# Attention of a graph network on one core: weighted sums in four banks, row weights copied to SBUF, carries in the scores bank, scores and chunk steps spaced two rounds apart

## Chip, cores and metric

The kernel runs on one core of one Trainium2 chip. The metric is device time in microseconds (us), lower is better; a kernel's time is the median of its runs.

## What is computed

Two graph networks run one after the other on 3125 nodes and 100000 edges, sorted by their target node. The first has two message layers. The second has three attention layers (GATv2, four heads of 32 channels), and the change lies there. Cut to what matters:

```python
gl = (x @ Wl + bl).reshape(n, HEADS, CH)
gr = (x @ Wr + br).reshape(n, HEADS, CH)
xj = gl[src]
e = jax.nn.leaky_relu(xj + gr[dst] + edge_e, negative_slope=0.2)
alpha = jnp.einsum('ehc,hc->eh', e, att_w)
m = jax.ops.segment_max(alpha, dst, num_segments=n)
alpha = jnp.exp(alpha - m[dst])
denom = jax.ops.segment_sum(alpha, dst, num_segments=n)
out = jax.ops.segment_sum(xj * (alpha / (denom[dst] + 1e-16))[..., None], dst, num_segments=n)
```

A batch norm over nodes and a leaky rectifier follow each layer.

## The kernel before

The edges are cut into 812 tiles of 128, each of which belongs to one block of 112 target nodes. Four tiles are a quad, so a layer has 203 quads (`NQ`). Two tiles are a pair. Up to eight quads are a chunk: `ENDS` has their ends, 27 chunks a layer. The softmax runs as an online one over chunks: maxima are found inside a chunk with scans, carried on from the chunk before, and the sums that were already added are rescaled when the maximum rises.

Every engine's program is written out by hand as a loop over rounds `j`, one quad a round, and waits on semaphores alone; nothing reorders it. `STEPS[c]` has the rounds of chunk c's steps 0 to 4 (scans, carries, args on DVE; an exponential on ACT; the transposed weights on PE), `PXR[i]` the round in which quad i is weighted. What a round j holds:

- POOL (L581) gathers the rows of a tile's source nodes from DRAM, one indirect DMA a tile. It may be up to eight quads ahead of PE (a wait on `s_e`).
- SP loads, every second round, the one-hot and edge columns of eight tiles (`ste_d`, L804, 512 KB), the one-hot rows of an earlier pair of quads (`nbb_d`, L767, 224 KB) and, once a chunk, its masks (L788, L789). It is held back by `s_e` too.
- PE, in this order: the chunk steps (L1393 and L1394, L1399 and L1400, L1408 to L1411); `scat` of the quad that was weighted two rounds ago, two pairs (L1360, into `PS[6]` and `PS[7]`); `pair` (a transpose L1372 and a multiplication L1374 a tile, into `PS[0]` or `PS[1]`); `scores` of the quad before (L1385, into `PS[2]` or `PS[3]` by the chunk's parity). Each fp32 multiplication is two instructions.
- ACT: the expanders of quad j+2 (L1036), the one-hot rows of the weighted quad (L1042), the scaled copy LE of quad j (L1047), which waits for `pair(j)` and for the scores of quad j-2, and the chunk's exponentials (L1052).
- DVE: an addition (L1959), the weight step of a quad (`weight`, L2028: the gathered rows times the weights, 528 elements a partition), a second addition, the chunk step that is due, the leaked step (L2036, which waits for LE), and the third and fourth addition. An addition adds a tile's sums from PSUM to its node block in SBUF; the four of a round belong to the quad that PE summed in that round.

So `scat` of pair v waits for the additions of pair v-2, whose bank it overwrites:

```python
w.wait_ge(s_acc2, pair_at(l, v_ - 2) if v_ >= 2 else 0)
for t in (2 * v_, 2 * v_ + 1):
    x = e.matmul(PS[6 + v_ % 2][0:B, (t % 2) * 132:(t % 2 + 1) * 132], SQ4[:, i % 4, t % 4, :],
```

and `pair(j)` waits for the leaked step of quad j-2. The carries' small products stand in `PS[5]`, the transposed weights of a chunk in `PS[4]`, which the weight step reads from there. DVE also reads the block numbers of 16 tiles into registers once every four rounds (L509). Layer 2 has 19 further DVE steps (`prepared`, from L2040 on), one every sixth round.

## Time and profile before

| | us |
|---|---|
| median of 3 runs | 8436.67 |
| lowest and highest run | 8432.65, 8437.69 |
| profiled execution: span | 8424.8 |
| DVE busy | 3907.3 (46%) |
| ACT busy | 3352.0 (40%) |
| POOL busy | 4643.3 (55%) |
| PE busy, by modelled ends | 5601.5 (66%) |

The span goes from the first to the last instruction; of the profiled execution no other time is given, and the median lies 11.9 us above it. Times in the rows are counted from the span's start. The three attention layers' rounds lie at 4330 to 5650, 5688 to 7019 and 7057 to 8390 us. PE is the matmul, PEld the weight load, PEclk the granted clock of TensorE as a share of 2.4 GHz (0.5 is 1.2 GHz), mean over the stretch. In a row of the timeline "x4" are four instructions merged, and the brackets give the idle time before them and what ended it; "remote" means that no instruction ended shortly before the semaphore rose. Ends of matmuls are modelled.

### The profile page before, as it was taken

The numbers are of one execution on the slowest core, as the hardware profiler recorded it, in microseconds if no ns is written. First come the engines' busy times: TensorE is split into PE (matmuls) and PEld (weight loads), VectorE is DVE, ScalarE is ACT, GpSimd is POOL, SyncE is SP. The second block draws the span as 40 slices with busy tenths as digits, with TensorE's granted clock in tenths as the row PEclk, the third lists the DMA queues.
The fourth block names the chain that finished last, engine by engine and source line by source line (L and its number), as shares of the span: only waits on it lengthen the run. The fifth ranks groups of instructions, "written<-read, shape, count | busy, mean of one in ns | idle before, by whom it ended". The sixth has DMA issues, their size and how long they took to land.

```text
span 8424.8 us, 124432 instructions
## 1 busy us (share of the span) xinstructions
PE 5601.5 (66%) x35700; PEld 4989.9 (59%) x35700; DVE 3907.3 (46%) x13770; ACT 3352.0 (40%) x12652; POOL 4643.3 (55%) x4868
## 2 busy tenths in 40 slices
PE   7445445577777767777747777775766765777666
PEld 5333333566666666666646666665666665666666
DVE  4221221466666566665644444452444443444445
ACT  2222222366666556666623333332333332333332
POOL 2555554366666356666536666626666653666652
PEclk9999999899999888888978888877888886888887
DMA  2000001344344234444323333323333332333332
GB/s 56 22 25 23 24 22 21 95 105 103 103 105 103 78 102 121 119 118 119 101 54 111 109 107 108 108 78 94 107 103 108 107 107 66 111 104 108 107 106 64
DMA packets 489686, 743.92 MB, mean 88 GB/s; under 512 B 219285, under 2 KB 351865, under 8 KB 487973
## 3 DMA queue, kind: packets, MB, share of 16 engines
q1 hardware_dynamic: 307764, 423.98, 16.2%
q0 software_dynamic: 180928, 305.59, 15.1%
q10 hardware_dynamic: 320, 6.40, 0.3%
q8 instruction: 296, 4.85, 0.2%
q14 instruction: 378, 3.10, 0.1%
HBM read 636.97 MB, written 97.83 MB: 87 GB/s over the span
## 4 chain that ended last, share of the span: by engine, by line
PE 19%; issue 14%; another core or an unknown queue 12%; DVE 11%; ACT 4%; DVEq 3%; ACTq 0%; POOL 0%; DMA 0%
PE PS L1360 5%; DVE AR L1959 5%; PE PS L1374 4%; PE PS L1250 2%; PE PS L1372 2%; PE PS L1274 2%; PE PS L1271 1%; DVEq L509 1%; ACT AR L1047 1%; DVE AR L1879 1%; PE PS L1385 1%; DVEq L1959 1%; ACT AR L1036 1%; DVE AR L1793 1%
## 5 line engine op out<-in xcount | busy, mean ns | idle before, releaser
L581 POOL DMA_INDIRECT AR<-gtab_d,AR x2436 | 2309.8, 948 | 1554.0 <-issue 604.9
L573 POOL DMA_INDIRECT AR<-ptab_d,AR x1624 | 1548.1, 953 | 1030.0 <-issue 395.2
L1047 ACT ACTIVATE AR<-PS,AR 128x512 f32<-128x512 f32 x609 | 418.4, 687 | 2551.1 <-remote 1319.7
L1360 PE MATMUL PS<-AR 128*112 128x132 f32 x4872 | 943.5, 335 | 651.1 <-DVE AR L1959 636.9
L1360 PEld LDWEIGHTS PS<-AR 128*112 128x112 f32 x4872 | 742.1, 212 | 798.2 <-DVE AR L1959 485.7
L1959 DVE TENSOR_TENSOR AR<-AR,PS 112x132 f32 x2436 | 695.9, 286 | 1011.8 <-issue 401.4
L555 POOL DMA_INDIRECT rec_d<-AR x782 | 760.0, 972 | 661.6 <-DVE AR L1555 437.8
L1374 PE MATMUL PS<-AR 128*128 128x128 f32 x4872 | 1058.1, 319 | 20.0 <-issue 19.5
L2036 DVE SCALAR_TENSOR_TENSOR AR<-PS,AR 128x512 f32<-128x512 f32 x609 | 455.7, 748 | 1201.5 <-issue 702.3
L1374 PEld LDWEIGHTS PS<-AR 128*128 128x128 f32 x4872 | 924.9, 236 | 23.2 <-issue 22.9
L1250 PE MATMUL PS<-AR 128*112 128x161 f32 x3248 | 672.5, 335 | 356.9 <-DVE AR L1879 216.6
L1385 PE MATMUL PS<-AR 128*128 128x128 f32 x4872 | 740.4, 298 | 152.3 <-DVE AR L2036 87.0
L950 ACT ACTIVATE AR<-PS 128x160 f32<-128x160 f32 x1624 | 493.6, 304 | 795.1 <-remote 334.2
L1271 PE MATMUL PS<-AR 112*128 x3248 | 789.7, 327 | 25.8 <-issue 25.4
L1879 DVE TENSOR_TENSOR AR<-AR,PS 112x161 f32 x1624 | 520.2, 320 | 618.0 <-issue 264.6
L1372 PE MATMUL PS<-ident,AR 128*128 128x128 f32 x2436 | 778.9, 320 | 40.6 <-DMA AR<-gtab_d,AR 20.8
L1274 PE MATMUL PS<-AR,ident 128*128 128x160 f32 x3248 | 777.9, 323 | 2.4 <-issue 2.4
L1385 PEld LDWEIGHTS PS<-AR 128*128 128x128 f32 x4872 | 683.1, 215 | 152.4 <-DVE AR L2036 93.4
L1250 PEld LDWEIGHTS PS<-AR 128*112 128x112 f32 x3248 | 526.6, 199 | 409.3 <-issue 390.9
L1103 PE MATMUL PS<-AR 128*56 128x168 bf16 (+3 forms) x1369 | 379.6, 432 | 461.3 <-DVE AR L1569 319.1
L1271 PEld LDWEIGHTS PS<-AR 112*128 112x128 f32 x3248 | 598.0, 212 | 43.0 <-issue 42.7
L1274 PEld LDWEIGHTS PS<-AR,ident 128*128 128x128 f32 x3248 | 595.1, 211 | 2.0 <-issue 1.9
(344 smaller groups left out, 8790.5 us busy)
## 6 DMA issues: line engine op xcount, KB each, us to landing
AR<-ste_d SPq DMA_DIRECT2D x404, 512.0 KB
AR<-nbb_d SPq DMA_DIRECT2D x303, 224.0 KB
ste_d<-AR SPq DMA_DIRECT2D x101, 512.0 KB
AR<-gtab_d,AR POOLq DMA_INDIRECT x2436
AR<-ptab_d,AR POOLq DMA_INDIRECT x1624
nbb_d<-AR SPq DMA_DIRECT2D x101, 224.0 KB
AR<-key_d SPq DMA_DIRECT2D x94, 224.0 KB
AR<-rec_d SPq DMA_DIRECT2D x812, 8.0 KB
```

The source lines that it names most:

```text
L555: e.indirect_dma_start(out=rec_d[:, :], out_offset=bass.IndirectOffsetOnAxis(ap=rowi[:, n:n + 1], axis=0), in_=REC[:, c * RW:(c + 1) * RW] ...
L573: e.indirect_dma_start(out=XJ1[:, t % 32, :], out_offset=None, in_=tabs_d[0][:, :], in_offset=off).then_inc(done_, 16)
L581: e.indirect_dma_start(out=xj2(t)[:, t % 4, :], out_offset=None, in_=tabs_d[1][:, :], in_offset=off).then_inc(done_, 16)
L1250: x = e.matmul(PS[4 + v_ % 2][0:B, (t % 2) * 161:(t % 2 + 1) * 161], SW[:, (t // 4) % 4, t % 4, :], VB[:, v_ % 6, t % 2, :], start=True, s ...
L1271: e.matmul(o, STE[0:B, ste_slot(l, t), (t % 8) * 128:(t % 8 + 1) * 128], TABQ[0:B, bass.ds(block_of(cp, "tensor", t), 1), :], start=True, ...
L1274: x = e.matmul(o, ident[:, :], XJ1[:, t % 32, :], start=False, stop=True, skip_group_check=True)
L1360: x = e.matmul(PS[6 + v_ % 2][0:B, (t % 2) * 132:(t % 2 + 1) * 132], SQ4[:, i % 4, t % 4, :], PX[:, i % 5, t % 4, :, :].rearrange("p c h - ...
L1372: e.transpose(o, xj2(t)[:, t % 4, 0:128], ident[:, :])
L1374: x = e.matmul(o, expander(t), STE[:, ste_slot(l + 2, t), (t % 8) * 128:(t % 8 + 1) * 128], start=False, stop=True, skip_group_check=True)
L1385: x = e.matmul(PS[2 + c % 2][:, 0:128], ATW[:, 31 - t:159 - t], LE[:, i % 2, kk * 128:(kk + 1) * 128], start=(t == 0), stop=(i == ENDS[c] ...
L1879: x = e.tensor_tensor(o, o, PS[4 + v_ % 2][0:B, (t % 2) * 161:(t % 2 + 1) * 161].unsqueeze(1), ALU.add)
L1959: x = e.tensor_tensor(o, o, PS[6 + v_ % 2][0:B, (t % 2) * 132:(t % 2 + 1) * 132].rearrange("p (a c h) -> p a c h", a=1, h=4), ALU.add)
```

## The change

Line numbers of the changed kernel differ by a few from those above (L1385 becomes L1388, L1360 L1363, L1372 L1375, L1374 L1377, L1959 L1960, L2028 L2037, L2036 L2045).

- `scat` writes to `PS[4]` to `PS[7]` in turn, and waits for the additions of pair v-4.
- The carries' products and the transposed weights go to the columns behind and over the scores in the chunk's scores bank `PS[2 + c % 2]`.
- The first weight step of a chunk copies the transposed weights to `PTT` and the rescaling factors to `RT`, both in SBUF, and gives the bank back through a new semaphore `s_tc`. `scores` waits for that instead of for the args of chunk c-2. All weight steps read `PTT`, the rescaling reads `RT`.
- `scores(j - 2)` stands at the end of round j, where `scores(j - 1)` stood.
- The rounds of the chunk steps: 9, 10, 11, 11, 12 for chunk 0 become 9, 11, 13, 13, 15, and so on every eight rounds. Quads are weighted 15 rounds behind their tiles' round where it was 12, and two a round near the end of a layer, where DVE calls `weight` twice. There are 26 chunks, and 215 rounds where there were 217.
- SP loads `nbb_d` two steps of its loop later.

```diff
-    ends = list(range(8, 185, 8)) + [190, 195, 199, NQ]
+    ends = list(range(8, 193, 8)) + [198, NQ]
...
-        back = max(turn + 3, px[-1] + 1 if px else 0)
-        steps.append((turn, turn + 1, turn + 2, turn + 2, back))
-        px += [back + i for i in range(end - start)]
+        back = turn + 6
+        for i in range(start, end):
+            back = max(back, px[-1] + 1 if px and (px[-1] < NQ or px[-2:] == [px[-1]] * 2) else px[-1] if px else 0)
+            px.append(back)
+        steps.append((turn, turn + 2, turn + 4, turn + 4, px[start]))
...
-                for g8 in range(NG + 7):
+                for g8 in range(NG + 9):
...
-                    w.wait_ge(s_acc2, pair_at(l, v_ - 2) if v_ >= 2 else 0)
+                    w.wait_ge(s_acc2, pair_at(l, v_ - 4) if v_ >= 4 else 0)
                     for t in (2 * v_, 2 * v_ + 1):
-                        x = e.matmul(PS[6 + v_ % 2][0:B, (t % 2) * 132:(t % 2 + 1) * 132], SQ4[:, i % 4, t % 4, :],
+                        x = e.matmul(PS[4 + v_ % 4][0:B, (t % 2) * 132:(t % 2 + 1) * 132], SQ4[:, i % 4, t % 4, :],
...
-                        w.wait_ge(s_arg, chunk_at(l, c - 2))
+                        w.wait_ge(s_tc, chunk_at(l, c - 2))
...
                         w.wait_ge(s_pt, chunk_at(l, c))
-                        w.wait_ge(s_rs, chunk_at(l, c - 1))
-                        w.wait_ge(s_px, quad_at(l, chunk_start(c) - 1))
-                        e.transpose(PS[4][:, 0:128], PT, ident[:, :])
+                        e.transpose(PS[2 + c % 2][:, 0:128], PT, ident[:, :])
...
-                    if 1 <= j <= NQ:
-                        scores(j - 1)
+                    if 2 <= j <= NQ + 1:
+                        scores(j - 2)
...
-                    w.wait_ge(s_r, chunk_at(l, chunk_of(i)))
+                    c = chunk_of(i)
+                    t0 = 4 * (i - chunk_start(c))
+                    if t0 == 0:
+                        w.wait_ge(s_r, chunk_at(l, c))
+                        if c or l:
+                            w.wait_ge(s_px, quad_at(l, i - 1))
+                            w.wait_ge(s_rs, chunk_at(l, c - 1))
+                        v(e.tensor_copy(RT, PS[2 + c % 2][0:B, 128:132]))
+                        done(e.tensor_copy(PTT, PS[2 + c % 2][:, 0:128]), s_tc)
+                        w.wait_ge(s_tc, chunk_at(l, c))
...
-                        PS[4][:, 0:128].rearrange("p (h t) -> p t h", h=4)[:, t0:t0 + 4, :].unsqueeze(2).to_broadcast([128, 4, 33, 4]),
+                        PTT.rearrange("p (h t) -> p t h", h=4)[:, t0:t0 + 4, :].unsqueeze(2).to_broadcast([128, 4, 33, 4]),
...
                     add()
+                    if len(quads) > 1:
+                        weight(quads[1])
```

PE, layer 0, around the small products of a chunk's carries, with the banks' numbers. Before:

```order
L1374 MATMUL PS0<-AR 128x128
L1385 MATMUL PS2<-AR 128x128 x4
L1399 MATMUL PS5<-ones,AR 128x1
L1400 MATMUL PS5<-ones,AR 128x1
L1360 MATMUL PS6<-AR 112x132 x2
L1360 MATMUL PS7<-AR 112x132 x2
L1372 MATMUL PS1<-ident,AR 128x128
```

With the change:

```order
L1377 MATMUL PS0<-AR 128x128
L1388 MATMUL PS2<-AR 128x128 x4
L1402 MATMUL PS3<-ones,AR 128x1
L1403 MATMUL PS3<-ones,AR 128x1
L1363 MATMUL PS4<-AR 112x132 x2
L1363 MATMUL PS5<-AR 112x132 x2
L1375 MATMUL PS1<-ident,AR 128x128
```

The small products moved from `PS5` to the chunk's scores bank `PS3`, and the two pairs of weighted sums of a round from `PS6` and `PS7` to `PS4` and `PS5` (the next round takes `PS6` and `PS7`).

DVE, layer 0, around the first weight step of a chunk (528 elements); the additions have 132, and an ISA row sets an address for the next. Before:

```order
L1959 ISA
L1959 TENSOR_TENSOR AR<-AR,PS6 112x132
L2028 TENSOR_TENSOR AR<-AR,PS4 128x528
L1959 ISA
L1959 TENSOR_TENSOR AR<-AR,PS6 112x132
L2036 SCALAR_TENSOR_TENSOR AR<-PS0,AR 128x512
```

With the change:

```order
L1960 ISA
L1960 TENSOR_TENSOR AR<-AR,PS4 112x132
L2032 COPY AR<-PS2 112x4
L2033 COPY AR<-PS2 128x128
L2037 TENSOR_TENSOR AR<-AR 128x528
L1960 ISA
L1960 TENSOR_TENSOR AR<-AR,PS4 112x132
L2045 SCALAR_TENSOR_TENSOR AR<-PS1,AR 128x512
```

Two copies from the scores bank stand ahead of the multiplication, and its second input is no longer in PSUM.

## Rows read from the trace of the kernel before

**Rows 1.** Timeline, layer 0: start us, us, engine, line and operation, tiles, count, idle before.
```profile
4999.56 0.64 PE L1374 MATMUL PS<-AR 128*128 128x128 f32 x2
...
4999.99 1.86 PE L1385 MATMUL PS<-AR 128*128 128x128 f32 x8
...
5000.36 0.69 ACT L1047 ACTIVATE AR<-PS,AR 128x512 f32<-128x512 f32 x1 [3.30 <-issue]
...
5001.08 0.75 DVE L2036 SCALAR_TENSOR_TENSOR AR<-PS,AR 128x512 f32<-128x512 f32 x1 [2.52 <-ACT AR L1047]
...
5002.18 0.29 DVE L1959 TENSOR_TENSOR AR<-AR,PS 112x132 f32 x1 [0.15 <-issue]
...
5002.53 0.70 PE L1360 MATMUL PS<-AR 128*112 128x132 f32 x4 [0.23 <-DVE AR L1959]
...
5004.18 0.39 PE L1374 MATMUL PS<-AR 128*128 128x128 f32 x2
...
5004.40 1.06 PE L1385 MATMUL PS<-AR 128*128 128x128 f32 x8
5006.95 0.29 DVE L1959 TENSOR_TENSOR AR<-AR,PS 112x132 f32 x1 [4.48 <-remote]
5007.04 0.69 ACT L1047 ACTIVATE AR<-PS,AR 128x512 f32<-128x512 f32 x1 [4.74 <-remote]
...
5009.59 0.29 DVE L1959 TENSOR_TENSOR AR<-AR,PS 112x132 f32 x1 [0.22 <-DVE AR L1959]
```

**Rows 2.** Waits of all engines: who for whom, us in total, times, longest us.
```profile
ACT AR L1047 <- remote: 1319.7, 279, 38.4
...
PE PS L1360 <- DVE AR L1959: 636.9, 384, 5.0
```

**Rows 3.** Waits of PE, the chunk steps.
```profile
PE PS L1408 <- ACT AR L1052: 129.7, 59, 5.4
...
PE PS L1393 <- DVE AR L1973: 102.4, 26, 4.6
```

**Rows 4.** Windows: us; busy of PE, PEld, DVE, ACT, POOL; PEclk, DMA share, GB/s.
```profile
4487.10:5600.10 1113.00, 813.99 (x5406) 755.41 (x5405) 512.12 (x1519) 364.57 (x1130) 664.99 (x702) 0.85 0.37 106
5600.10:5650.20 50.10, 35.37 (x160) 29.87 (x158) 30.15 (x100) 9.34 (x19) 0.00 (x0) 0.60 0.23 68
5847.80:6969.40 1121.60, 795.05 (x5405) 734.36 (x5404) 510.21 (x1518) 364.68 (x1130) 663.03 (x700) 0.86 0.37 105
7213.40:8338.00 1124.60, 793.06 (x5406) 730.41 (x5405) 522.80 (x1538) 365.03 (x1130) 667.23 (x702) 0.87 0.37 105
```

**Rows 5.** Windows with L1372 alone: us; busy and count of PE, PEld.
```profile
4487.10:5600.10 1113.00, 232.37 (x728) 124.75 (x729) 0.85 0.37 106
```

**Rows 6.** Timeline of POOL, start of layer 1.
```profile
5706.30 0.95 POOL L581 DMA_INDIRECT AR<-gtab_d,AR  x1 [0.30 <-issue]
...
5732.56 0.95 POOL L581 DMA_INDIRECT AR<-gtab_d,AR  x1 [0.30 <-issue]
```

**Rows 7.** Timeline, layer 2, around a DVE step with both inputs in SBUF.
```profile
7483.23 0.95 POOL L581 DMA_INDIRECT AR<-gtab_d,AR  x1 [0.30 <-issue]
...
7483.77 1.08 DVE L2048 TENSOR_TENSOR AR<-AR 112x896 f32<-112x896 f32 x1
...
7484.48 1.20 POOL L581 DMA_INDIRECT AR<-gtab_d,AR  x1 [0.30 <-issue]
```

**Rows 8.** Timeline of DVE, the carries and args of one chunk.
```profile
5019.70 0.27 DVE L1983 COPY AR<-PS 1x128 f32<-1x128 f32 x1
...
5022.01 0.15 DVE L2004 TENSOR_TENSOR AR<-AR 1x4 f32<-1x4 f32 x1
...
5025.56 0.15 DVE L2011 COPY AR<-PS 128x2 f32<-128x2 f32 x1
...
5026.92 0.29 DVE L2020 TENSOR_TENSOR AR<-PS,AR 128x128 f32<-128x128 f32 x1
```

**Rows 9.** Chain of waits, 5016 to 5019 us: start us, us, what.
```profile
5017.42 1.10 DVEq L509
```

More of the change, by code:

```diff
@@ L222, in gnn_program @@
         NW, FD, FR = carve(4, 1), carve(4, 1), carve(4, 1)
+        PTT, RT = carve(128), carve(4, B)
         assert cur[0] <= AREA - 4 * T - TK - NB, cur[0]
@@ L380, in gnn_program @@
             sem(n) for n in ("s_ex", "s_s0", "s_v", "s_car", "s_c", "s_arg", "s_pt", "s_f", "s_r"))
-        s_px, s_oh2, s_scat2, s_acc2, s_rs = (sem(n) for n in ("s_px", "s_oh2", "s_scat2", "s_acc2", "s_rs"))
+        s_px, s_oh2, s_scat2, s_acc2, s_rs, s_tc = (sem(n) for n in ("s_px", "s_oh2", "s_scat2", "s_acc2", "s_rs", "s_tc"))
         s_cnt, s_lk, s_k4, s_kx, s_mk = (sem(n) for n in ("s_cnt", "s_lk", "s_k4", "s_kx", "s_mk"))
@@ L758, in sync_program @@
                             load_masks(e, w, l, c)
-                    o8 = g8 - 7
+                    o8 = g8 - 9
                     if o8 >= 0:
@@ L1392, in tensor_program @@
                         w.wait_ge(s_s0, chunk_at(l, c))
-                        e.matmul(PS[5][0:1, 128:256], SS[:, 0:1], ident[:, :], start=True, stop=True, skip_group_check=True)
-                        done(e.matmul(PS[5][0:1, 256:384], SS[:, 127:128], ident[:, :], start=True, stop=True, skip_group_check=True), s_v)
+                        e.matmul(PS[2 + c % 2][0:1, 128:256], SS[:, 0:1], ident[:, :], start=True, stop=True, skip_group_check=True)
+                        done(e.matmul(PS[2 + c % 2][0:1, 256:384], SS[:, 127:128], ident[:, :], start=True, stop=True, skip_group_check=True), s_v)
                     c = step_of(j, 2)
@@ L1398, in tensor_program @@
                         w.wait_ge(s_car, chunk_at(l, c))
-                        e.matmul(PS[5][:, 384:385], GL_, ones[0:1, 0:1], start=True, stop=True, skip_group_check=True)
-                        done(e.matmul(PS[5][:, 385:386], GE_, ones[0:1, 0:1], start=True, stop=True, skip_group_check=True), s_c)
+                        e.matmul(PS[2 + c % 2][:, 384:385], GL_, ones[0:1, 0:1], start=True, stop=True, skip_group_check=True)
+                        done(e.matmul(PS[2 + c % 2][:, 385:386], GE_, ones[0:1, 0:1], start=True, stop=True, skip_group_check=True), s_c)
                     c = step_of(j, 4)
@@ L1405, in tensor_program @@
                         w.wait_ge(s_pt, chunk_at(l, c))
-                        w.wait_ge(s_rs, chunk_at(l, c - 1))
-                        w.wait_ge(s_px, quad_at(l, chunk_start(c) - 1))
-                        e.transpose(PS[4][:, 0:128], PT, ident[:, :])
+                        e.transpose(PS[2 + c % 2][:, 0:128], PT, ident[:, :])
                         w.wait_ge(s_f, chunk_at(l, c))
-                        e.matmul(PS[4][0:B, 128:132], MR[:, mask_slot(l, c), 512:624], FR, start=True, stop=False, skip_group_check=True)
-                        done(e.matmul(PS[4][0:B, 128:132], MR[:, mask_slot(l, c), 624:736], ones[0:1, 0:4],
+                        e.matmul(PS[2 + c % 2][0:B, 128:132], MR[:, mask_slot(l, c), 512:624], FR, start=True, stop=False, skip_group_check=True)
+                        done(e.matmul(PS[2 + c % 2][0:B, 128:132], MR[:, mask_slot(l, c), 624:736], ones[0:1, 0:4],
                                       start=False, stop=True, skip_group_check=True), s_r)
@@ L1978, in carries @@
                     g4, e4 = GL_.rearrange("p (h t) -> p h t", h=4), GE_.rearrange("p (h t) -> p h t", h=4)
-                    v0, v1 = PS[5][0:1, 128:256], PS[5][0:1, 256:384]
+                    v0, v1 = PS[2 + c % 2][0:1, 128:256], PS[2 + c % 2][0:1, 256:384]
                     w.wait_ge(s_v, chunk_at(l, c))
@@ L1983, in carries @@
                     v(e.tensor_copy(vr[:, :, 1:33], v1.rearrange("p (h t) -> p h t", h=4)))
-                    ends_ = v(e.tensor_tensor(BE_, PS[5][0:1, 129:257], r[:, 256:384], ALU.add))
+                    ends_ = v(e.tensor_tensor(BE_, PS[2 + c % 2][0:1, 129:257], r[:, 256:384], ALU.add))
                     add()
@@ L2010, in args @@
                     w.wait_ge(s_v, chunk_at(l, c))
-                    columns = v(e.tensor_copy(CC, PS[5][:, 384:386]))
+                    columns = v(e.tensor_copy(CC, PS[2 + c % 2][:, 384:386]))
                     add()
```

7 lines of the change are left out of this document (3 added, 4 removed).

## The prediction

> **What bounds the kernel now.** I read the waits first, then the timeline of a few rounds, then windows over whole layers. The waits [rows 2] name the place: TensorE (PE) stood idle for 636.9 us, in 384 waits, before the weighted sums L1360, until VectorE (DVE) had done an addition L1959. The biggest entry of all is ACT's: 279 of its 609 LE steps (L1047) waited 1319.7 us for something "remote".
>
> The timeline [rows 1] shows both inside one loop. The pair's last multiplications L1374 start at 5004.18 and end at 5004.57; the LE step starts at 5007.04, so PE's completion reached ACT 2.5 us late, and DVE's addition at 5006.95 had waited as long. This is what "remote" stands for. One round earlier the same step was prompt: L1374 ended at 5000.20, LE started at 5000.36. From there LE to the leaked step L2036 takes 0.72 us, from that to the end of the fourth addition 1.39 (5001.08 to 5002.47), and at once, at 5002.53, PE starts the second pair of sums. PE cannot run ahead: with two banks the second pair of sums of a round needs the additions behind the previous round's leaked step. So one round closes a loop: sums, pairs, LE, leaked, additions, sums.
>
> The pace: a window with L1372 alone [rows 5] holds 728 of them, four a round, so 182 rounds; the three middles of the layers [rows 4] take 1113.0 + 1121.6 + 1124.6 = 3359.2 us for 546 rounds, **6.15 us a round**. In them no engine is full: POOL 665 of 1113, DVE 512, PE 814 by modelled ends. The floor under it: when nothing holds POOL, gathers start 26.26 us apart over 21 gathers [rows 6], 1.25 each, **5.0 us a round** of four.
>
> **The change, part by part.**
>
> *Four banks.* Sums of pair v wait for the additions of v-4, so both pairs of a round need only additions of two rounds before. The 636.9 us [rows 2] lose their cause; what is late next is this loop over two rounds, at full clock: second sums, pairs and scores on PE 2.93 us (5002.53 to 5005.46 [rows 1]); lateness of the completion, 279 of 609 times some 2.5 and otherwise 0.16, mean 1.23; LE to leaked 0.72; leaked to the fourth addition's end 1.39. Together 6.3 us for two rounds. No instruction is added or removed here.
>
> *Scores two rounds behind.* Same instructions, later. PE no longer waits at its round's end for the leaked step of the round before. But LE(j) may overwrite its buffer only after scores(j-2), and these now stand behind pair(j): every LE starts at the scores' end, 0.9 us behind the pair's end (5005.46 against 5004.57), and at half clock 1.65 (5001.85 against 5000.20). I have put the scores inside the 2.93, so this new wait is paid. Behind LE on ACT are the next expanders, wanted by PE only three rounds later: hidden.
>
> *Chunk steps two rounds apart, carries in the scores bank.* PE waited at L1408 129.7 us and at L1393 102.4 [rows 3], because ACT and DVE had one round for a step. Now they have two; I take these waits as gone. The scores bank is given back at the first weight step of the chunk, round 8c+15, and wanted by the scores of chunk c+2 in round 8c+18: three rounds of cover, 15 us. If the cover were gone, PE would wait once a chunk for DVE. On DVE the steps stay, before the leaked step: carries 5019.70 to 5022.16, args 5025.56 to 5027.21 [rows 8], 2.46 + 1.65, the scans taken like the args, 5.8 a chunk. Twice a chunk the block numbers are loaded to registers, 1.10 each [rows 9].
>
> *Row weights copied to SBUF.* Two DVE copies a chunk and one own wait. The copy at 5019.70 took 0.27 [rows 8]; two of them and a gap make 0.2 to 0.8, I take 0.5, hidden in DVE's slack: 78 chunks, 39 us of work that counts only if DVE becomes the bound. The multiplication itself keeps its 528 elements; its second input now comes from SBUF. A row for that form is the added step L2048: 896 elements with both inputs in SBUF took 1.08 us, and the gather that POOL started inside it took 1.20 us against 0.95 [rows 7]. So each of the 609 multiplications may cost POOL between nothing and 0.25 us; with POOL short of being the bound it costs nothing, and I take nothing. The Trainium skill, page "SBUF — State Buffer", section "Who interferes with whom", has a rule that speaks against the change here: a DVE instruction with two SBUF inputs contends with a GpSimd instruction that reads SBUF. By that rule the fastest outcome would be 7968 us instead of 7832 (both worked out below), and the forecast stays, since its pace lies above both. By that rule, the trace agrees in the one place shown.
>
> *Weighted sums three rounds later, two a round at the end.* After the last tile round 15 quads remain where 12 did. Before, this tail took 50.1 us (from 5600.1 to 5650.2 [rows 4]). DVE needs 2.64 us a quad when it never waits (5006.95 to 5009.59 [rows 1]), so 3 x 2.64 x 3 layers = +24 us; bounds 0 (the doubled rounds hide each other's waits) and 24. On SP the nbb load comes two pairs of rounds later and a mask load one; they are issued behind the same loads of ste_d, at least three rounds before use: hidden. One chunk fewer a layer (27 to 26) saves about 6 us of DVE work each, hidden as well, taken as 0.
>
> **The sum.** At full clock: the two-round loop 6.3, the chunk's work on DVE (5.8 + 0.5 + 2.2) / 8 x 2 = 2.1, together 8.4, or 4.2 a round: below POOL's 5.0, so POOL sets the pace. At half clock PE's own work decides: 28 instructions a round at 0.213 us (two from 4999.56 to 4999.99 [rows 1]) are 5.96, with ten small ones a chunk 6.2. The granted clock is 0.85 to 0.87 [rows 4], so some 30% of the time is at 1.2 GHz and the rest at 2.4. With that share kept: 0.7 x 5.0 + 0.3 x 6.2 = 5.36, taken as **5.4 us a round**. Saved: 546 x (6.15 - 5.4) = 411 us. I leave the first 20 rounds of each layer as they are, and add 24 for the tail. The profiled span 8424.8 becomes 8038; the median of the runs lies 11.9 above the span, so **8050 us**.
>
> **The rivals.**
>
> 1. *POOL's pace throughout.* The eight quads that POOL is ahead even out the half-clock rounds: 5.0 a round, 8437 - 629 + 24 = 7832 us. For it: 702 gathers at 1.25 are 878 of the 1113 us, so POOL lacks little, and PE would be busy without long gaps, which may hold 2.4 GHz. Against: completions 2.5 us late stay. 0.19.
> 2. *POOL's pace, lengthened by the multiplications from SBUF.* Each of the 609 holds one gather for up to 0.25 us: 5.25 a round, 7968 us. For it: the 1.20 us gather. Against: a gather is held only if it starts while the multiplication runs. The page named above has this rule. 0.10.
> 3. *The late completions take the place of the bank wait.* They hold ACT, DVE and POOL at once; if DVE cannot catch up in between (it has 2.64 + 1.1 of work a round, more in chunk steps), the pace ends near 5.8: 8437 - 192 + 24 = 8268 us. 0.17.
> 4. *Nothing moves.* The LE step behind the scores gives back what the banks free: 6.15 a round, 8437 to 8460 us. 0.05.
> 5. *Slower: PE at half clock.* In the middles PE works in bursts and is granted 0.85 to 0.87; in the tail, where its work is thin, 0.60 [rows 4]. If PE's work, spread evenly, is granted 1.2 GHz all along, PE is the bound in its own order, at 6.24 a round with nothing lost between: +48 + 24, 8509 us. It decides once more than 90% of the time is at 1.2 GHz, a PEclk under 0.55 in the middles. Against: such a PE has no gaps, and behind gapless work the level went from half to full between 5001.85 and 5002.53 [rows 1]. 0.09.
>
> **How the numbers follow.** Forecast 0.40 (5.2 to 5.6 a round, 7940 to 8160), rivals 0.19, 0.10, 0.17, 0.05, 0.09. A measurement of this kernel tells some 0.2% (17 us) from no change. Faster by more: 0.40 + 0.19 + 0.10 + 0.17 = 0.86. Rival 4 mostly stands within: same 0.04, slower 0.10. The range leaves out rivals 4 and 5 and a little at each end: its low end is rival 1 with the first rounds quickened too (36 rounds x 1.15 = 41 less), 7790; its high end a pace of 5.85, 8300.
>
> **What the profile after would show.** Right: the wait of L1360 for L1959 below 150 us, the chunk steps' waits on PE below 60; "remote" before the LE step still there; 728 transposes in about 980 us; gathers 1.25 apart in full-clock stretches; PEclk not under 0.85. Rival 1 shows as gathers 1.25 apart through the middles, rival 2 as gathers of 1.2 us beside the multiplications, rival 3 as DVE and ACT idle together for "remote" while PE waits for the additions again, rival 5 as PEclk near 0.5. The forecast is wrong in its main step if PE still waits for DVE's additions for more than 400 us.

## The result, and the profile after

The changed kernel took **8347.51 us** (median of 4 runs, 8335.14 to 8353.35) against 8437.18 of the kernel before on the same chip (4 runs, 8432.65 to 8448.02): ratio **0.9886, 95% interval 0.9874 to 0.9898**. That is 1.1% faster. The forecast was 8050 us, and its range ended at 8300.

Lines have moved by the edit: the sums L1360 are L1363 now, the transposes L1372 are L1375, the pair's multiplications L1374 are L1377, the scores L1385 are L1388, the additions L1959 are L1960, the weight step L2028 is L2037, the leaked step L2036 is L2045, LE L1047 is L1050, the gathers L581 are L584.

The costliest groups on the page of the changed kernel, its first line with them:

```profile
span 8333.0 us, 124313 instructions
...
L584 POOL DMA_INDIRECT AR<-gtab_d,AR x2436 | 2583.5, 1061 | 1193.9 <-issue 673.3
...
L1050 ACT ACTIVATE AR<-PS,AR 128x512 f32<-128x512 f32 x609 | 417.9, 686 | 2337.3 <-remote 1777.0
...
L2037 DVE TENSOR_TENSOR AR<-AR 128x528 f32<-128x528 f32 x609 | 654.8, 1076 | 2.9
```

Its waits of PE (us, times, longest), which answer to [rows 2, 3]:

```profile
PE PS L1363 <- issue: 298.0, 366, 2.5
...
PE PS L1363 <- DVE AR L1960: 68.4, 91, 2.1
...
PE PS L1409 <- ACT AR L1055: 20.3, 17, 2.8
...
PE PS L1396 <- DVE AR L1974: 2.8, 4, 1.3
```

Windows over the same stretches as [rows 4] (first transposes of quads 20 to 202 of each layer, and one tail); the columns are those of [rows 4]:

```profile
4479.60:5567.30 1087.70, 833.76 (x5398) 750.54 (x5396) 581.40 (x1551) 366.38 (x1136) 766.14 (x707) 0.81 0.39 109
5567.30:5628.30 61.00, 40.43 (x196) 35.10 (x194) 45.29 (x132) 11.34 (x24) 0.00 (x0) 0.65 0.22 63
5817.80:6902.00 1084.20, 843.91 (x5398) 757.64 (x5397) 580.85 (x1551) 366.17 (x1136) 757.34 (x706) 0.82 0.39 110
7150.70:8235.40 1084.70, 827.49 (x5398) 746.84 (x5397) 589.78 (x1564) 365.50 (x1136) 753.89 (x705) 0.82 0.38 110
```

What these show. The waits for the additions fell from 636.9 us to 68.4, and PE's wait for ACT's exponential from 129.7 to 20.3, as meant. But the middles went only from 3359.2 to 3256.6 us, 5.96 us a round for 6.15. Three things grew that no instruction count explains. Two are durations: the weight step's multiplication, from 697 ns (the group of L2028 on the page of the kernel before) to **1076 ns** at the same 528 elements, and the gathers, from 948 to **1061 ns** on average.

The third is idle time of PE for which the profile shows no releaser ("issue"). PE's waits from 4450 to 5600 us, in layer 0, before the change and after it:

```profile
PE PS L1360 <- DVE AR L1959: 201.6, 113, 4.0
PE PS L1408 <- ACT AR L1052: 31.7, 16, 2.6
PE PS L1399 <- issue: 26.7, 14, 2.1
```

```profile
PE PS L1363 <- issue: 101.7, 121, 2.5
PE PS L1377 <- issue: 48.3, 88, 1.7
PE PS L1375 <- issue: 32.1, 46, 2.6
PE PS L1388 <- issue: 22.8, 44, 1.1
PE PS L1363 <- DVE AR L1960: 17.6, 21, 2.1
```

Summed over the three middles, PE's idle time put down to VectorE or ScalarE fell from 847 us to 57, and the idle time without a releaser rose from 103 to **680**. Some of those 680 us are still waits for other engines, since only 818 of the additions' 1218 semaphore updates are in this trace: 128 us end right behind an instruction of VectorE or ScalarE. But 385 us, in 588 gaps, stand ahead of instructions that wait for no semaphore at all; before the change that was 37 us in 50. PE stands still between its own instructions.

The time by stretch: middles -103, first twenty rounds of the three layers -21, tails, from the last such transpose to the last addition (49.7, 49.5, 50.1 before, 61.1, 58.8, 61.1 after) +32: together -92, and the spans differ by 91.8.

A timeline of the changed kernel shows a held gather and a late completion within four microseconds: a gather that starts inside a multiplication takes twice its time (5013.19), and LE starts 1.59 us behind the recorded end of the scores it waits for (5012.92 to 5014.51, "remote"):

```profile
5011.23 1.69 PE L1388 MATMUL PS<-AR 128*128 128x128 f32 x8
...
5011.95 0.94 POOL L584 DMA_INDIRECT AR<-gtab_d,AR  x1 [0.30 <-issue]
...
5013.16 1.08 DVE L2037 TENSOR_TENSOR AR<-AR 128x528 f32<-128x528 f32 x1
5013.19 1.88 POOL L584 DMA_INDIRECT AR<-gtab_d,AR  x1 [0.30 <-issue]
...
5014.51 0.69 ACT L1050 ACTIVATE AR<-PS,AR 128x512 f32<-128x512 f32 x1 [1.95 <-remote]
```

### The profile page after: what moved, and what is told of

It reads as the page before. It is cut to its first block, busy times and chain, and to the rows that moved or that the text cites. A ratio compares the mean times of both kernels' runs of the same rounds, so it can differ in the third digit from the quotient of the medians.

```text
span 8333.0 us, 124313 instructions
## 1 busy us (share of the span) xinstructions
PE 5688.3 (68%) x35659; PEld 5004.8 (60%) x35659; DVE 4136.5 (50%) x13855; ACT 3352.7 (40%) x12645; POOL 4908.0 (59%) x4868
## 4 chain that ended last, share of the span: by engine, by line
PE 30%; issue 13%; another core or an unknown queue 8%; DVE 7%; ACT 4%; DVEq 1%; ACTq 0%; DMA 0%; POOL 0%
PE PS L1363 7%; PE PS L1377 6%; PE PS L1388 6%; PE PS L1375 3%; PE PS L1253 2%; PE PS L1277 1%; PE PS L1274 1%; DVE AR L1880 1%; DVE AR L1960 1%; ACT AR L1039 1%; DVE AR L1794 1%; ACT AR L953 1%; DVE AR L1889 1%; ACT AR L1050 1%
## 5 line engine op out<-in xcount | busy, mean ns | idle before, releaser
L584 POOL DMA_INDIRECT AR<-gtab_d,AR x2436 | 2583.5, 1061 | 1193.9 <-issue 673.3
L1050 ACT ACTIVATE AR<-PS,AR 128x512 f32<-128x512 f32 x609 | 417.9, 686 | 2337.3 <-remote 1777.0
L1377 PE MATMUL PS<-AR 128*128 128x128 f32 x4872 | 1097.2, 320 | 152.7 <-issue 148.1
L1363 PE MATMUL PS<-AR 128*112 128x132 f32 x4872 | 898.1, 318 | 386.4 <-issue 298.0
L1377 PEld LDWEIGHTS PS<-AR 128*128 128x128 f32 x4872 | 923.4, 232 | 214.1 <-issue 212.4
L2045 DVE SCALAR_TENSOR_TENSOR AR<-PS,AR 128x512 f32<-128x512 f32 x609 | 455.0, 747 | 1159.9 <-ACT AR L1050 910.5
L1960 DVE TENSOR_TENSOR AR<-AR,PS 112x132 f32 x2436 | 692.2, 284 | 654.3 <-PE PS L1363 246.6
L1363 PEld LDWEIGHTS PS<-AR 128*112 128x112 f32 x4872 | 720.3, 203 | 483.6 <-issue 378.2
L1375 PE MATMUL PS<-ident,AR 128*128 128x128 f32 x2436 | 769.9, 316 | 252.9 <-issue 133.7
L1388 PE MATMUL PS<-AR 128*128 128x128 f32 x4872 | 819.5, 312 | 113.1 <-issue 109.2
L1388 PEld LDWEIGHTS PS<-AR 128*128 128x128 f32 x4872 | 741.9, 227 | 144.7 <-issue 141.5
L1253 PEld LDWEIGHTS PS<-AR 128*112 128x112 f32 x3248 | 520.6, 197 | 408.0 <-issue 388.7
L2037 DVE TENSOR_TENSOR AR<-AR 128x528 f32<-128x528 f32 x609 | 654.8, 1076 | 2.9
```

Of the source, the lines that this page charges most:

```text
L584: e.indirect_dma_start(out=xj2(t)[:, t % 4, :], out_offset=None, in_=tabs_d[1][:, :], in_offset=off).then_inc(done_, 16)
L1253: x = e.matmul(PS[4 + v_ % 2][0:B, (t % 2) * 161:(t % 2 + 1) * 161], SW[:, (t // 4) % 4, t % 4, :], VB[:, v_ % 6, t % 2, :], start=True, s ...
L1363: x = e.matmul(PS[4 + v_ % 4][0:B, (t % 2) * 132:(t % 2 + 1) * 132], SQ4[:, i % 4, t % 4, :], PX[:, i % 5, t % 4, :, :].rearrange("p c h - ...
L1375: e.transpose(o, xj2(t)[:, t % 4, 0:128], ident[:, :])
L1377: x = e.matmul(o, expander(t), STE[:, ste_slot(l + 2, t), (t % 8) * 128:(t % 8 + 1) * 128], start=False, stop=True, skip_group_check=True)
L1388: x = e.matmul(PS[2 + c % 2][:, 0:128], ATW[:, 31 - t:159 - t], LE[:, i % 2, kk * 128:(kk + 1) * 128], start=(t == 0), stop=(i == ENDS[c] ...
```

## The experiments

Theories: (1) PE itself is the bound, 28 instructions at 0.213 us being just 5.96; (2) the longer multiplications and gathers eat the gain; (3) PE's completions come late by a fixed delay a round; (4) the LE step's new wait for the scores eats it. Variants have letters: 1b says that the gathers set the pace where PE completes promptly, 1c that PE with its halts is the bound where it does not. The runs fell on several chips, and that turned out to matter more than any edit: on one the kernel before took 8367 us, on four others 6731 to 6735, a fifth less, with the same instructions. I call them **slow chips** (the first one, 8437, and that one) and **quick chips**. Whether it is the chip or its condition at that hour is not shown: each of the two slow chips was met once. Ratios are always to the kernel before on the same chip.

**PE by itself, quick chip.**

> TensorE by itself: six sections of 20 groups of 28 fp32 instructions (A 128x128 weights and 128 columns, B transposes, C 112 rows and 132 columns, D 4 columns, E the mix of one round of the attention loop, F one weight tile for all), each group's end told by a semaphore to a one-column ScalarE activation, whose starts show when groups are really complete; the output is a copy of the input and nothing of the reference is computed. Theory 1 (TensorE sustains one fp32 instruction in about 0.213 us whatever granted clock the rows show, since 5.96 us a round in the changed kernel is 28 x 0.213): the groups of E complete 5.96 us apart, although rows of single matmuls may start 0.11 us apart. Theory 2 (the extra time of the vector multiplication and the gathers, 1076 against 697 ns and 1061 against 948 ns, sets the pace, and TensorE has room): groups of E complete about 28 x 0.11 to 28 x 0.13, 3.1 to 3.7 us apart, at a high granted clock.

The whole took 441.3 us. At a granted clock of 1.0 a group in the round's mix (E) ended every 3.13 us, 0.112 an instruction; the section with four moving columns was granted 0.5 and took 5.97 us a group, 0.213. So 0.213 is the price at 1.2 GHz and no hidden limit. Theory 1 in its first form does not hold on such a chip.

**Scores issued twice, and a third LE buffer, quick chip.**

```diff
-                        for kk in range(4):
+                        for kk in (0, 0, 1, 1, 2, 2, 3, 3):
```

> The changed kernel with every scores matmul issued twice (the scores come out doubled, so the output differs), 8 TensorE instructions more a round, 36 for 28. Theory 1 (TensorE is the bound at 0.213 us an instruction): 8 x 0.213 = 1.70 us more a round, x 609 rounds = about 1040 us, 9385 us in all (9250 to 9450). Theory 2 (GpSimd and the vector port set the pace, 5.44 us a round of gathers within 5.96): TensorE has room at 0.11 to 0.12 us an instruction, under 100 us more. Theory 3 (late completions: a fixed delay in each round): about 8 x 0.11 x 609 = 540 us more.

```diff
-        LE = carve(2 * 512).rearrange("p (g n) -> p g n", g=2)
+        LE = carve(3 * 512).rearrange("p (g n) -> p g n", g=3)
...
-                        if j >= 2:
-                            w.wait_ge(s_lin, quad_at(l, j - 2))
+                        if j >= 3:
+                            w.wait_ge(s_lin, quad_at(l, j - 3))
```

> The changed kernel with a third buffer for the activations LE, so that the activation of round j waits for the scores of round j-3 and no longer for those of j-2, which now stand behind the pair of round j. Theory 1 (TensorE bound): within 20 us of the changed kernel, 8330 to 8370. Theory 4 (this wait, 378 waits and 1777 us idle of ScalarE in the changed kernel, holds the loop): the start of the activation comes back from 5.4 us to about 1.7 us behind the pair's end and the pace falls towards 5.44 us a round, -250 to -320 us, about 8060 us.

Measured: 7050.3 and 7023.9 us, where the change itself takes 7028.8 (below). Eight more PE instructions a round cost 21 us in all, and LE starting at once behind the pair gains nothing. PE and the LE wait are not the bound there. The first number is what theory 2 asked (under 100 us more), and the gain that theory 4 asked of the second is absent.

**Three banks, weights read from PSUM.** PS[4] to PS[6] hold the sums, PS[7] the transposed weights, and the copy is gone:

```diff
-                    w.wait_ge(s_acc2, pair_at(l, v_ - 4) if v_ >= 4 else 0)
+                    w.wait_ge(s_acc2, pair_at(l, v_ - 3) if v_ >= 3 else 0)
...
-                        PTT.rearrange("p (h t) -> p t h", h=4)[:, t0:t0 + 4, :].unsqueeze(2).to_broadcast([128, 4, 33, 4]),
+                        PS[7][:, 0:128].rearrange("p (h t) -> p t h", h=4)[:, t0:t0 + 4, :].unsqueeze(2).to_broadcast([128, 4, 33, 4]),
```

> The changed kernel with three banks for the weighted sums and the transposed weights kept in the eighth bank of PSUM and read from there, no copy to SBUF. Theory 2 (two SBUF inputs of the vector multiplication against GpSimd): the multiplication falls from 1076 to about 700 ns and the gathers from 1061 to about 950 ns, and the time falls with the gathers by up to 4 x 0.11 x 609 = 270 us, to about 8080. Theory 1 (TensorE bound): the two durations fall in the same way, and the time stays within 30 us of the changed kernel, 8320 to 8380.

It ran four times, each on a quick chip (6745, 6746, 6736, 6741 us): ratios 1.0017, 1.0016, 1.0013 and 1.0016, the last 1.0006 to 1.0027. Both durations fell as expected, the multiplication to 696 ns and the gathers to 948. The theories differed in the time, and on a quick chip it fell by 284 us against the change's 7028.8 (below), near the 270 of theory 2.

**The change itself, on a quick chip**, was run late, on the same chip as the fourth of those:

> The changed kernel unaltered, which has so far run only where the kernel before takes 8437 or 8367 us (ratios 0.989 and 0.985). Where the kernel before takes 6733 us: gathers back to back, 0.951 us where no multiplication overlaps them and 1.33 where one does, 4 x (1.07 + 0.305) = 5.5 us a round, 7025 to 7060 us, ratio 1.045, its neighbours with one edit having taken 7024, 7040 and 7062. Where it takes 8367 or more: 0.985 to 0.989 again.

7028.84 us against 6731.02: **1.0447, 1.0425 to 1.0469. On this quick chip the change is 4.5% slower.** Windows over 182 rounds of layer 0, of the change and then of the three-bank kernel:

```profile
3518.10:4512.40 994.30, 762.58 (x5397) 697.97 (x5395) 579.15 (x1548) 367.58 (x1136) 773.36 (x726) 0.89 0.44 121
```

```profile
3517.20:4424.10 906.90, 717.30 (x5397) 657.50 (x5396) 502.15 (x1502) 367.12 (x1136) 685.92 (x725) 0.94 0.47 133
```

Gathers: 773.36 / 726 = 1.065 us, with 0.305 between them, (994.30 - 773.36) / 726; 4 x 1.37 = 5.48 a round, and the window has 5.46. Of the three-bank kernel: 0.946 + 0.305, 5.0, and 4.98. POOL is the bound from end to end in both. PE's waits for gathered rows say the same, first in the change on this quick chip, then in the change on the first, slow one:

```profile
PE PS L1375 <- DMA AR<-gtab_d,AR: 817.9, 700, 6.9
```

```profile
PE PS L1375 <- DMA AR<-gtab_d,AR: 26.2, 26, 6.7
```

On the slow chip the rows lie ready. From the end of a quad's last gather instruction to PE's first transpose of that quad it is 34 us on average and never under 19 in the middles (32 and 12 on the second slow chip), where it is 0.0 us on average on the quick one. POOL is 6.5 quads ahead of PE there and 1.1 here, and in the slow middle of layer 0 it is POOL that waits, 105 us, for PE (L1377 or "remote"). So the gathers set the pace on quick chips, and on slow chips they do not.

The timeline on the quick chip shows the price again, and LE prompt behind the scores' end, 4002.54:

```profile
4000.44 1.07 DVE L2037 TENSOR_TENSOR AR<-AR 128x528 f32<-128x528 f32 x1
4000.71 1.63 POOL L584 DMA_INDIRECT AR<-gtab_d,AR  x1 [0.30 <-issue]
...
4001.48 1.06 PE L1388 MATMUL PS<-AR 128*128 128x128 f32 x8
...
4002.63 0.69 ACT L1050 ACTIVATE AR<-PS,AR 128x512 f32<-128x512 f32 x1 [3.41 <-PE PS L1388]
```

Over the whole trace, the 790 gathers that overlap a multiplication take 1.286 us and the other 1646 take 0.951.

**The copy alone, slow chip (8367 us).**

```diff
+                        v(e.tensor_copy(RT, PS[4][0:B, 128:132]))
+                        done(e.tensor_copy(PTT, PS[4][:, 0:128]), s_tc)
...
-                        PS[4][:, 0:128].rearrange("p (h t) -> p t h", h=4)[:, t0:t0 + 4, :].unsqueeze(2).to_broadcast([128, 4, 33, 4]),
+                        PTT.rearrange("p (h t) -> p t h", h=4)[:, t0:t0 + 4, :].unsqueeze(2).to_broadcast([128, 4, 33, 4]),
```

> The kernel before with one part of the change alone: the transposed weights and the carry's factor are copied from their PSUM bank to SBUF, and the vector multiplications read them there; two banks for the sums, and all steps as before. Theory 2 (two SBUF inputs of the multiplication hold up GpSimd's gathers): the multiplication takes 1076 us for 697 ns, the gathers 1.06 to 1.07 for 0.95 us. Where gathers stand back to back that is 4 x 0.12 x 609 = 290 us more, +4.3%, 7025 us; where the kernel before takes 8437 us, its slack of 0.29 us behind each gather takes it up, and the time moves by less than 100 us. Without that contention: no difference on either.

(The first "us" behind 1076 stands for ns.) Multiplication 1077 ns, gathers 1054 on average; time 8393.59 us, ratio 1.0025 (1.0006 to 1.0043). So the copy alone brings both prices; in a kernel whose gathers have slack they cost 26 us (5 to 36).

**The change and the kernel before again, and PE alone, on that slow chip.**

> The changed kernel unaltered. The last four runs shared a chip on which the kernel before took 6733 us, not 8437, and TensorE by itself completed 28 instructions in 3.13 us. Theory 1b (two limits: where TensorE completes promptly, the gathers set the pace in every case, and the change makes each gather 0.12 us longer, 4 x (1.07 + 0.305) = 5.5 us a round against 4 x (0.948 + 0.305) = 5.0): on such a chip the changed kernel takes about 7030 us, 4.4% over the kernel before. Where the kernel before takes 8437 us again, the ratio of the first comparison, 0.989, comes again. Theory 3 (the time of the change is the same on both chips): 0.989 on either.

> The kernel before, unaltered, for its profile beside the others of this call. Theory 1b: on a chip with 6733 us its gathers stand back to back, 0.95 us and 0.305 us apart, 5.0 us a round, and the two-round loop through the sums of TensorE and the additions of VectorE, 6.3 us a round on the first chip, does not hold it; where it takes 8437 us, the profile is that of before, 6.15 us a round.

> TensorE by itself once more, the same six sections (nothing of the reference is computed). On a chip where the kernel before takes 6733 us: 3.13 us for 28 instructions at full clock, 5.97 at half, as before. On a chip where it takes 8437 us, theory 1 (TensorE by itself sustains less there, whatever clock the rows show): 5.9 us or so at a granted clock near 1; theory 5 (TensorE alone is as quick there, and something beside it, DMA or the other engines, delays its completions): 3.13 us again.

8252.84 us, ratio 0.9851 (0.9832 to 0.9871): the first result came again, a little larger. The kernel before shows the trace of [rows 1 to 4] again, 6.14 us a round. PE alone took 441.5 us, with the same 3.13 and 5.97 us a group: by itself PE is as quick on a slow chip. Inside the kernels it is not. In a window of 900 us from 4500 on, the share of PE's recorded semaphore updates that come over 0.5 us behind the last recorded end of an instruction that makes them is 45% in the kernel before and 59% in the change on this chip (41% and 68% on the first one), and none in the change on a quick chip. The median late one is 1.8 to 3.1 us behind. In the first 200 us of the program a fifth of the updates are late already, long before the attention layers. The idle time of PE without a releaser is there again too, 714 us in the change's middles for 48 in those of the kernel before.

**PE beside the other engines.**

> TensorE with the instruction mix of one round (28 fp32 instructions a group, 40 groups a section; nothing of the reference is computed), eight sections: alone; beside VectorE multiplications; beside ScalarE activations; beside GpSimd gathers; beside SyncE's 512 KB loads; beside all four; with a wait for its own semaphore after each group, alone; and so beside all four. On a chip where the kernel before takes 8350 to 8440 us, TensorE's semaphores come up to 13 us late in half to three quarters of the updates. Theory 5a (the halts come with the power or traffic of the other engines): no halts alone, halts of 2 to 7 us in one or more of the sections beside others, which names the engine. Theory 5b (the halts come where TensorE stops and starts): they show in the two sections with waits and in no other. Theory 5c (neither): 3.13 us a group in all. On a chip where the kernel before takes 6733 us: 3.13 us a group in all sections without the wait.

> TensorE with the instruction mix of one round, eight sections of 40 groups: alone; beside VectorE; beside ScalarE; beside GpSimd's gathers; beside SyncE's loads; beside all four; waiting for its own semaphore after each group, alone; and so beside all four (nothing of the reference is computed). On the chip where the kernel before takes 6734 us it took 1039 us in all with no late semaphore. On a chip where the kernel before takes 8350 to 8440 us: theory 5a (the halts come with the power or traffic of other engines): halts of 2 to 7 us in one or more of the sections beside others and none alone, 1100 to 1500 us in all. Theory 5b: only in the two sections with waits. Theory 5c (neither, something that these sections do not have): 1039 us again.

Both runs fell on quick chips: 1038.8 and 1040.1 us, 3.13 us a group in all sections without the wait and 3.44 in the two with it. What brings the halts on slow chips was not reached by them and stays open. One row answers another question: its multiplications have two contiguous SBUF operands of the size of L2037, and gathers beside them,

```profile
L89 POOL DMA_INDIRECT G<-in_x,idx x270 | 254.9, 944 | 754.3 <-PE PS L48 382.9 <-ACT A L116 290.0 <-issue 81.4
L103 DVE TENSOR_TENSOR V<-VI 128x528 f32<-128x528 f32 x330 | 205.8, 704 | 762.0 <-PE PS L48 762.0
```

take 704 and 944 ns, also where both run. Two SBUF operands alone are not what costs 1076.

**The copy laid out the other way, quick chip.** The same copy, with the four heads of a tile side by side:

```diff
-                        done(e.tensor_copy(PTT, PS[2 + c % 2][:, 0:128]), s_tc)
+                        done(e.tensor_copy(PTT.rearrange("p (t h) -> p t h", h=4), PS[2 + c % 2][:, 0:128].rearrange("p (h t) -> p t h", h=4)), s_tc)
...
-                        PTT.rearrange("p (h t) -> p t h", h=4)[:, t0:t0 + 4, :].unsqueeze(2).to_broadcast([128, 4, 33, 4]),
+                        PTT.rearrange("p (t h) -> p t h", h=4)[:, t0:t0 + 4, :].unsqueeze(2).to_broadcast([128, 4, 33, 4]),
```

> The changed kernel with the copy to SBUF laid out by tile and head instead of by head and tile (the copy itself reads PSUM with the stride), so that the multiplication reads four neighbouring elements at a time instead of elements 128 bytes apart; nothing else is altered. In the runs so far a multiplication of two contiguous SBUF operands of the same 128x528 size took 701 to 707 ns beside gathers of 944 ns, while the change's own takes 1080 ns and the gathers that overlap it 1332 ns (951 where they don't), so theory 2c (the stride of the SBUF operand, not its being in SBUF, costs the 380 ns and holds up GpSimd) expects 700 ns and gathers of 0.95 us: where the kernel before takes 6733 us, 6735 to 6760 instead of about 7030; where it takes 8367, 7950 to 8050 if the gathers hold the changed kernel there, 8200 to 8250 if TensorE with its halts does. Theory 2 (two SBUF inputs as such, or the broadcast): 1076 ns and 1.07 us stay, and the time stays at about 7030 or 8253.

6855.57 us, ratio 1.0186 (1.0165 to 1.0207), neither of the two values expected. Its groups:

```profile
L584 POOL DMA_INDIRECT AR<-gtab_d,AR x2436 | 2421.3, 994 | 864.2 <-issue 715.5
...
L2037 DVE TENSOR_TENSOR AR<-AR 128x528 f32<-128x528 f32 x609 | 426.3, 701 | 2.9
```

The multiplication is back at 701 ns, so its 370 to 380 ns were all stride; the gathers that overlap it still take 1.106 us for 0.949. So the change's price on a quick chip has two parts: of its +298 us the stride makes some 173 (7029 to 6856), and the gathers still held make most of the rest, which the contiguous multiplication did not show. Whether that comes from the broadcast operand or from something else that the kernel has and that small program lacks was not tested.

**Half the scores, and two banks, quick chip.**

> The changed kernel with two of the four scores matmuls of each round left out (the attention scores are wrong, 24 TensorE instructions a round for 28). Where the kernel before takes 6733 us and the gathers stand back to back: no change, 7030 us. Where it takes 8367: theory 1c (TensorE with its halts is the bound, 5.9 us for 28 instructions, halted a third of the time): 4 x 0.21 = 0.84 us a round less until the gathers' 5.53 bound it, so 5.55 us a round, -210 us, 8040 us. Theory 4 (the wait of the activation for the scores holds the loop): -4 x 0.11 x 609 = -270 us at most, through the same line. Theory 2 (gathers alone bound it): within 40 us of 8253.

Then two banks:

```diff
-                    w.wait_ge(s_acc2, pair_at(l, v_ - 4) if v_ >= 4 else 0)
+                    w.wait_ge(s_acc2, pair_at(l, v_ - 2) if v_ >= 2 else 0)
...
-                        x = e.matmul(PS[4 + v_ % 4][0:B, (t % 2) * 132:(t % 2 + 1) * 132], SQ4[:, i % 4, t % 4, :],
+                        x = e.matmul(PS[6 + v_ % 2][0:B, (t % 2) * 132:(t % 2 + 1) * 132], SQ4[:, i % 4, t % 4, :],
```

> The changed kernel with two banks for the sums again, the wait for the additions of the pair before the last back; the copy to SBUF, the later scores and the later chunk steps stay. Where the kernel before takes 8367 us: the step of the prediction (four banks take away 637 us of waits of TensorE, up to 0.9 us a round) says 8253 + 250 to 400; if TensorE's halts absorb the waits, as the changed kernel's gain of 1.5% suggests, +50 to +120 us, 8300 to 8370. Where it takes 6733: 7030, no change, since the gathers bound both.

7039.69 us (one run): PE's work is free there. Two banks took 7061.73, ratio 1.0488 (1.0471 to 1.0506). The wait for the additions is all there again,

```profile
PE PS L1363 <- DVE AR L1960: 636.7, 590, 2.8
```

and it costs 33 us against the 7028.84 of the change, measured on another chip. That the total is that of before the change [rows 2] is chance: it is 590 waits here and 384 there, on a slow chip. A wait of the engine that is not the bound has its full size in the list and next to no price.

**The banks alone.** The kernel before with a third bank for the sums and the edge rows and carries in the scores bank; nothing else:

```diff
-                    w.wait_ge(s_acc2, pair_at(l, v_ - 2) if v_ >= 2 else 0)
+                    w.wait_ge(s_acc2, pair_at(l, v_ - 3) if v_ >= 3 else 0)
...
-                        x = e.matmul(PS[6 + v_ % 2][0:B, (t % 2) * 132:(t % 2 + 1) * 132], SQ4[:, i % 4, t % 4, :],
+                        x = e.matmul(PS[(4, 6, 7)[v_ % 3]][0:B, (t % 2) * 132:(t % 2 + 1) * 132], SQ4[:, i % 4, t % 4, :],
```

> The kernel before with one part of the change alone, as far as it goes without the copy: a third bank for the sums (the wait of TensorE for the pair two earlier becomes one for the pair three earlier), got by moving the edge rows and carry columns into the bank of the scores; weights read from PSUM, scores one round behind and chunk steps one round apart as before. Where the kernel before takes 6733 us and the gathers stand back to back: no change, 6720 to 6750. Where it takes 8367 or 8437: if TensorE's waits for the additions are the limit there (theory of the prediction), the gathers' slack of 0.29 us each closes in large part, -150 to -350 us, 8020 to 8220 of 8367; if its halts are (theory 1c), the waits only change their name, 0 to -100 us.

A quick chip once more: 6728.1 us, ratio 0.9990 (0.9981 to 1.0000). The tail took 48.2 us in layer 0, against 56.1 in the three-bank kernel with the later chunk steps, so the later steps cost about 8 us a layer in the tail. The third and fourth runs of the three-bank kernel asked about slow chips,

> Three banks for the sums, transposed weights read from PSUM, no copy, the later scores and chunk steps of the change kept: the same kernel as twice before, 6745 us on a chip where the kernel before takes 6734 us. Where the kernel before takes 8367 us: theory 2b (the copy's longer gathers and multiplications are what holds the changed kernel at 5.93 us a round, 5.53 of it gathers): the gathers fall to 0.948 us and the pace towards 5.4 to 5.5, -250 to -300 us against the changed kernel's 8253, 7950 to 8000. Theory 1c (TensorE with its halts is the bound at 5.9): 8230 to 8290.

> Three banks, transposed weights read from PSUM, no copy, the later scores and chunk steps kept. Where the kernel before takes 6733 us: 6736 to 6746, as three times before. Where it takes 8367 or more: theory 2b (the copy's longer gathers hold the changed kernel at 5.93 us a round): 250 to 300 us under the changed kernel of the same call. Theory 1c (TensorE with its halts holds it): within 40 us of it.

and got a quick chip's 6735.94 and 6741.34 (the second run had asked the same, and got 6745.80). No kernel tried beats the kernel before on a quick chip by more than the measurement tells: those that read the weights from PSUM end at POOL's 5.0 us a round.

## Why the prediction was wrong

Point by point, by its own steps:

- *Four banks: the 636.9 us lose their cause.* The wait went, 68.4 left, under the 150 that it named. The time did not go with it.
- *Chunk steps' waits gone.* Right: 20.3 us for ACT and 2.8 for DVE remain of 129.7 and 102.4.
- *"4.2 a round: below POOL's 5.0, so POOL sets the pace"*, in the 70% of the time at full clock. **This is the step that failed.** On this chip POOL never set the pace: it stood 6.5 quads ahead of PE, and PE waited for gathered rows 26.2 us in the whole kernel. PE itself set it. In the three middles PE was busy 2505 us by modelled ends, idle 680 us with no releaser shown and idle 57 us for VectorE and ScalarE; that is 3242 of the 3256.6 us, or 4.6, 1.24 and 0.10 us a round. The sum had no term for the 1.24. It counted a late completion once in a loop of two rounds, at 1.23 us on average, and put PE's own standing still at nothing.
- *Where the 411 us went.* In the middles the profile shows 790 us less of PE waiting for other engines. 576 us came back as idle time without a releaser (up to 128 of them unrecorded waits, as said above), and 103 us as longer work of PE, whose granted clock fell from a range of 0.85 to 0.87 to one of 0.81 to 0.82. What is left over is about the 103 us that the middles gained. Either the wait for the additions had stood over a delay that PE has anyway on such a chip, or the change itself makes PE stand still more; the traces do not tell, and the cause stays open.
- *POOL's floor at 5.0 us a round.* Right where gathers take 0.948 us and PE completes promptly: three-bank kernels run at 4.98 to 5.03 on quick chips.
- *"The multiplication itself keeps its 528 elements"*, with its time taken as unchanged, and *"I take nothing"* for the gathers. Wrong too, and decisive on quick chips. The multiplication took 1076 ns, and the gathers gained 2583.5 - 2309.8 = 273.7 us, 0.45 for each multiplication, over the upper bound of 0.25. In the middle of layer 0 a gather takes 766.14 / 707 = 1.084 us, so POOL's floor rose to 4 x (1.084 + 0.305) = 5.55. It lies under the 5.96 measured here; with it the prediction's own sum gives 0.7 x 5.55 + 0.3 x 6.2 = 5.75, so it would explain two thirds of the miss at most. That it cost little on the slow chips is what the rows lying ready say, and the copy alone, which cost 26 us there. The longer multiplication can also delay PE through VectorE, but of that PE's waits show 57 to 185 us in all. On a quick chip the gathers are the bound, and their length makes the 298 us (7028.8 against 6731.0) but for the 10 that the three-bank kernel has too.
- *Tail +24.* Measured +32; on the slow chip the copy alone made a tail of 56.4 us from 49.0, so it has a share in this too.
- *PEclk not under 0.85.* Wrong: 0.81 and 0.82. It is far from the 0.55 at which rival 5 would decide.
- *First twenty rounds unchanged.* They gained 21 us.

Of the rivals, 3 came nearest: it had the late completions set a pace of 5.8 and a time of 8268 us. LE started a median 1.7 us behind the recorded end of the scores, 0.10 on a quick chip. The idle time before LE put down to "remote" rose from 1319.7 to 1777.0 us. But that rival's sign, PE waiting for the additions again, did not come, and the pace was slower still. Rival 2 had the contention of the gathers, at half its size; it decides on quick chips, for which no time was forecast.

The rule quoted in the prediction asks that a two-input multiplication contend with a GpSimd instruction that reads SBUF. The trace agrees in the kernels (1.106 against 0.949 us with the quick layout) and not beside the contiguous operands (944 ns in all sections). A second observation bears more: an SBUF operand read with a stride, at 1067 to 1080 ns in every kernel here that has it, costs half again as much as the same operand with neighbouring elements, 701, while PSUM took the strided pattern at 697. The Trainium skill, page "SBUF — State Buffer", section "Door 1: The DMA port swizzle", says that SBUF reads run at full bandwidth only within lines of 16 bytes, four fp32 elements, and pay for each crossing. By that rule, the trace agrees: head-major weights put each element 128 bytes from the next, tile-major ones fill a line. No run here used another stride, so the 16 bytes themselves are not shown.

What stays open: what makes PE stand still and complete late on some chips inside this kernel, when alone it does not; what three banks with weights in PSUM would bring there (the rows that lie ready speak for theory 1c, little or nothing, but no such run fell on a slow chip); and what still holds the gathers when the operand is laid out in fours.

## What to carry to other kernels

Before an operand is moved from PSUM to SBUF, price its access pattern and not its element count: a stride that is free in one memory can cost half again in the other, and it is paid twice if GpSimd issues gathers meanwhile. Before a wait is counted as a gain, ask whether the engine that waits is itself late: here the wait for the additions went, and most of its time came back as idle time of PE that nobody else ends. Look at who is ahead of whom, too: a producer that is six quads ahead is not the bound, however busy it is. When a wait is taken away, work out the new floor with the edit's own side effects in it. And time a change on more than one chip where the profile shows completions behind their recorded ends: here the same edit was 1.1% and 1.5% faster on two chips and 4.5% slower on a third.

## What the runs showed of the hardware

- Chips, or their condition at the hour, differ: the same kernel takes 8437 and 8367 us on two and 6731 to 6735 on four, with the same instructions. On the first two 41% to 68% of PE's semaphore updates in the attention layers come over 0.5 us late, and none on a quick one, at a granted clock in the records of 0.88 against 0.94 on average (the kernel before).
- A PE waiting list is no price list: 637 us of waits cost 33 us where POOL is the bound, and on a slow chip 790 us of waits less in the middles gained 103.
- A trace can lack semaphore updates: on the slow chip 6401 of VectorE's 10704 are recorded in the change, on the quick one 10626, so "issue" and "remote" on a slow chip hold some waits for other engines.
- At a granted clock of 1.0, 28 fp32 instructions with changing weights take 3.13 us, and nothing that VectorE, ScalarE, GpSimd or the loads did beside them changed that by 0.01 us on a quick chip.
